# A four-layer graph and mixture-of-experts kernel: x loaded transposed for the first GNN, its second weights applied last

## The reference, cut to what matters

```python
x = x + _L0_gnn_ref(_layernorm(x), adj, adj, W_proj, b_proj, W_gcn, b_gcn)
#   filt = tanh(adj * adj) * (adj > 0)      the 350 largest of each row stay
#   h2   = tanh(h @ W_proj + b_proj)
#   feat = relu(new_adj @ (h2 @ W_gcn) + b_gcn)
x = x + _L0_ffn_ref(_layernorm(x)[None], Wg, bg, bias, W1, b1, W2, b2)[0]
#   gate_logits = x_flat @ Wg + bg + bias   the two best of 8, softmax of the two
#   h = relu(x W1 + b1);  y = h W2 + b2;  weighted sum over the experts
x = x + _L1_gnn_ref(_layernorm(x), adj, L1_gnn_w)
#   deg = sum(adj + I, axis=1), used as deg ** -0.5
```

## Time and profile before

| | us |
|---|---|
| runs of the kernel | 576.0, 575.85, 572.77 (median 575.85) |
| the profiled execution | 571.83 |
| its span, first to last instruction | 570.1 |
| busy in the span: TensorE, VectorE, ScalarE, GpSimd | 487.1, 427.9, 314.2, 252.3 |

### The profile page before, as it was taken

One profiled execution on the slowest core, in us unless ns is written; L12 is line 12 of the kernel. 1 busy time (PEld: TensorE's weight loads), 2 busy tenths in 40 slices (PEclk: granted clock), 3 DMA queues, 4 the chain that ended last, 5 costly groups with the idle time before them and its releaser, 6 DMA issues.

```text
span 570.1 us, 11302 instructions
## 1 busy us (share of the span) xinstructions
PE 487.1 (85%) x3819; PEld 275.4 (48%) x3819; DVE 427.9 (75%) x1065; ACT 314.2 (55%) x522; POOL 252.3 (44%) x275
## 2 busy tenths in 40 slices
PE   1999995879999979998867778889989987898990
PEld 1533333557777745454432233233343226797990
DVE  6897966878999992565778679879977614866674
ACT  0687796966999900120113544456639654466770
POOL 3000002522444440110146189789946575377663
PEclk9999998989999999999957689999999996899996
DMA  8999975200115925011023443200040395869985
GB/s 293 400 422 423 421 274 178 93 1 22 30 28 203 409 58 115 0 42 28 15 75 99 122 118 104 90 2 1 0 143 20 135 356 160 250 182 361 399 299 186
DMA packets 39570, 93.43 MB, mean 164 GB/s; under 512 B 7488, under 2 KB 24944, under 8 KB 35168
## 3 DMA queue, kind: packets, MB, share of 16 engines
q1 hardware_dynamic: 35072, 86.96, 43.4%
q0 software_dynamic: 2272, 4.69, 2.3%
q10 hardware_dynamic: 2176, 1.13, 0.7%
HBM read 69.39 MB, written 21.00 MB: 159 GB/s over the span
## 4 chain that ended last, share of the span: by engine, by line
PE 54%; DVE 20%; DMA 9%; ACT 6%; issue 6%; SPq 3%; POOL 2%; POOLq 0%; DVEq 0%; ACTq 0%
PE ps L1586 9%; DVE A L2393 8%; PE ps L1763 8%; PE ps L1497 7%; PE ps L1514 6%; PE ps L1401 5%; PE ps L1755 3%; DMA R<-in_adj_in 3%; PE ps L1664 3%; DMA A<-w_split 2%; PE ps L1867 2%; PE ps L1611 2%; SPq L812 1%; PE ps L1381 1%; DMA slots_in<-R,A 1%
## 5 line engine op out<-in xcount | busy, mean ns | idle before, releaser
L2393 DVE TENSOR_REDUCE A<-ps 128x1 f32<-128x512 f32 (+3 forms) x160 | 86.1, 601 | 12.3 <-PE ps L1664 11.5
L1302 ACT ACTIVATE A<-ps 128x1024 f32<-128x1024 f32 (+3 forms) x80 | 68.4, 893 | 38.4 <-PE ps L1755 38.2
L1007 POOL TENSOR_TENSOR G<-G,A 128x1024 f32<-128x1024 f32 (+3 forms) x40 | 73.7, 1876 | 8.3 <-ACT A L1302 8.2
L1664 PE MATMUL ps<-A 96*128 96x512 f16 (+3 forms) x160 | 55.1, 382 | 10.3 <-DVE A L2393 4.5
L1401 PE MATMUL ps<-R,G 128*128 128x512 f32 x128 | 59.3, 605 | 1.2 <-DVE G L1967 0.8
L1586 PE MATMUL ps<-A,G 128*128 128x512 f32 x128 | 59.9, 594 | 0.0
L1514 PE MATMUL ps<-R 128*128 128x128 f16 x768 | 49.1, 221 | 7.0 <-DVE x L2085 5.8
L1514 PEld LDWEIGHTS ps<-R 128*128 128x128 f16 x768 | 46.1, 99 | 14.5 <-issue 6.6
L2067 DVE SCALAR_TENSOR_TENSOR R<-R 128x512 f16<-128x512 f32 x64 | 46.7, 752 | 6.8 <-ACT R L1157 6.5
L1867 PE MATMUL ps<-A 128*128 128x128 f16 (+1 forms) x702 | 47.6, 224 | 3.3 <-DMA A<-w_split 3.3
L1155 ACT ACTIVATE R<-ps,b 128x512 f32<-128x512 f32 x64 | 44.0, 688 | 10.6 <-PE ps L1497 9.4
(11 more groups left out here) (311 smaller groups left out, 920.7 us busy)
## 6 DMA issues: line engine op xcount, KB each, us to landing
A<-w_split SPq DMA_DIRECT2D x39, 533.0 KB, 10.2
A<-in_adj_t SPq DMA_DIRECT2D x16, 1024.0 KB, 17.6
slots_in<-xn SPq DMA_DIRECT2D x1, 8320.0 KB, 22.4
R<-in_adj_in SPq DMA_DIRECT2D x7, 1024.0 KB
w_split<-A SPq DMA_DIRECT2D x9, 725.0 KB, 4.0
xn<-in_adj_in SPq DMA_DIRECT2D x5, 1024.0 KB, 12.9
xT<-in_adj_in SPq DMA_DIRECT2D x4, 1024.0 KB, 12.6
A<-in_f_w SPq DMA_DIRECT2D x16, 170.5 KB
```

Source lines behind the costliest of these rows:

```text
L1007: pool.tensor_tensor(total, total, probabilities(n, pair)[:, :, t0:CW], ALU.add).then_inc(s_sum, 1)
L1302: act.activation(probabilities(n, pair)[:, :, t0:CW], ps[:, 2 * pair:2 * pair + 2, t0:CW], ACT.Exp, scale=1.0 / (SQ * SQ * float(HD) ** 0. ...
L1664: last = pe.matmul(ps[:, bank, 0:width], queries(t // TPC, h)[0:KQ, P * (t % TPC):P * (t % TPC) + P], keys(b, h // (NH // NKV))[0:KQ, 0:wi ...
L2393: dve.reduce_max(pm[:, h, t % TPC, b:b + 1], ps[:, bank, 0:width], AX_X).then_inc(s_rmf, 1)
```

## The change

Transposed x (`x_t`, from the host) is loaded beside x, both by chunks, and only chunk 0 precedes adjacency tile 0 on SP's queue; the others go behind tiles 0 to 2. The first layer norm is folded into the projection: the mean by centring the weights' columns (one product with ones, one VectorE instruction), the inverse root by a per-row factor behind the product, so that rows are no longer normalised or transposed there. The aggregation takes h2 itself; the second weights are multiplied behind it, in place of the transposition of the features, and their bias enters as three bf16 parts through one product. The ReLU moves into VectorE's addition. Later chunks' statistics and projections go between the tiles. The narrow operands come in one array, the others in three, issued behind tile 0's tanh. Only 12 row tiles are loaded and summed on ScalarE (10 in the aggregation, two behind it); the degrees of the last four come from TensorE, products with ones over all 16 adjacency tiles, placed in eight groups in the first expert turn and ahead of it, then a copy, a transposition and a copy. In the first turn ScalarE copies outputs 0 and 1 out of their banks (`save_output`), and VectorE's order is written out.

```diff
@@ SP
-            for g in range(NC):
+            def load_x(g):
                 sp.dma_start(x[:, w, :], x_in[:, w, :]).then_inc(s_x[g], 16)
+            def load_transposed_x(g):
+                sp.dma_start(raw_xT[:, CW * g:CW * g + CW], x_t[:, CW * g:CW * g + CW]).then_inc(s_xt[g], 16)
             def load_rows(i):
+                if row_buffer(i) == 2 and i < 3:
+                    sp.wait_ge(s_h2p, 1 + NC)
+                elif i >= 3:
+                    sp.wait_ge(s_rs, 1 + max(k for k in range(i) if row_buffer(k) == row_buffer(i)))
+            ROWS_BEHIND = {4: (0,), 6: (1,), 7: (2,), 9: (3,), 11: (4,), 12: (5,), 14: (6,), 15: (7, 8, 9, 10, 11)}
+            load_x(0)
+            load_transposed_x(0)
             for j in range(NT):
                 sp.dma_start(A[:, j, :], adj_t[j]).then_inc(s_A[j], 16)
+                if j + 1 < NC:
+                    load_x(j + 1)
+                    load_transposed_x(j + 1)
...
-            load_rows(NT - 2)
-            load_rows(NT - 1)
@@ ACT
+            SUMS_BEHIND = {4: (0,), 6: (1,), 7: (2,), 9: (3,), 11: (4,), 12: (5,), 13: (6,), 14: (7,), 15: (8, 9)}
+            FEATURES_BEHIND = {0: 0, 3: 1, 7: 2, 11: 3}
             for j in range(NT):
                 act.activation(fbuf[:, j % FB, :], fbuf[:, j % FB, :], ACT.Tanh).then_inc(s_F, 1)
+                if j in FEATURES_BEHIND:
+                    features_in(FEATURES_BEHIND[j])
+                if j == 0:
+                    for dst, src in small:
+                        act.dma_start(dst, src).then_inc(s_small, 16)
...
             features(s_feat)
-            row_sums(EARLY_ROWS)
+            row_sums(10)
+            row_sums(11)
...
+            scalar_rows(0)
+            high_parts(0)
+            scalar_rows(1)
+            HIGH_BEHIND = {(0, 0): 1, (0, 1): 2, (1, 0): 3}
...
                 if gg == 3:
+                    save_output(0)
+                    act.wait_ge(s_deg, 1)
+                    act.activation(late_sums, ps[:, DEGREE_BANK, 0:P], ACT.Copy).then_inc(s_degr, 1)
+                    save_output(1)
-                    row_sums(NT - 1)
@@ PE
+            pe.wait_ge(s_const, 1)
+            warm(6)
+            pe.wait_ge(s_first, 16)
+            pe.matmul(ps[:, 0, 0:P], full_ones, wmat[:, 0, :], start=True, stop=True).then_inc(s_h2p, 1)
+            def projection(g):
+                pe.wait_ge(s_xt[g], 16)
+                for q in range(TPC):
+                    last = pe.matmul(ps[:, 4 + g, P * q:P * q + P], raw_xT[:, P * (TPC * g + q):P * (TPC * g + q) + P], wmat[:, 0, :],
+                                     start=True, stop=True)
+                last.then_inc(s_h2p, 1)
+            warm(2)
+            pe.wait_ge(s_h2, 1)
+            projection(0)
+            warm(5)
+            projection(1)
+            warm(6)
...
             for j in range(NT - 1):
+                if j in (2, 4):
+                    projection(1 + j // 2)
+                if j % TPC == 0:
+                    pe.wait_ge(s_G, j // TPC + 1)
...
+                    last = pe.matmul(ps[:, 6 + g % 2, P * q:P * q + P], xT[:, P * t:P * t + P], wmat[:, 1, :],
+                                     start=False, stop=True, skip_group_check=True)
...
+            def late_degrees(tiles):
+                for j in tiles:
+                    for c in range(TPC):
+                        last = pe.matmul(ps[32 * c:32 * c + 32, DEGREE_BANK, 0:P], ones[:, :], A[:, j, P * (ROWS + c):P * (ROWS + c) + P],
+                                         start=(j == 0), stop=(j == NT - 1), skip_group_check=True)
...
             rows_back(2)
+            late_degrees(range(0, 2))
+            rows_back(3)
+            late_degrees(range(2, 4))
             rows_again(0)
-            rows_back(3)
-            rows_again(1)
+            late_degrees(range(4, 7))
...
+                if first_turn and SAVED <= gg < 2 * SAVED:
+                    pe.wait_ge(s_saved, gg - SAVED + 1)
@@ DVE
+            def scaled_projection(g):
+                for q in range(TPC):
+                    last = dve.scalar_tensor_tensor(out=G[:, t, :], in0=ps[:, 4 + g, P * q:P * q + P], scalar=rstd[:, t:t + 1],
+                                                    in1=proj_bias, op0=ALU.mult, op1=ALU.add)
...
+            AHEAD_OF = {3: ("scaled", 1), 6: ("stats", 2), 7: ("scaled", 2), 10: ("stats", 3), 11: ("scaled", 3)}
...
+                dve.scalar_tensor_tensor(out=rows(x, g), in0=ps[:, 6 + g % 2, :], scalar=0.0, in1=rows(x, g), op0=ALU.max,
+                                         op1=ALU.add).then_inc(s_x1, 1)
...
+            low(0, 0)
+            low(0, 1)
+            gate_logits()
+            low(0, 2)
+            pick(chain, dve, 1, lg[:, 5], lg)
...
+            add_from_bank(0, 2)
+            low(0, 4)
+            add_from_bank(1, 3)
+            low(0, 5)
+            add_saved(2, 0)
+            add_from_bank(3, 4)
+            low(0, 6)
+            add_saved(4, 1)
+            add_bias2(0, 5)
+            add_from_bank(5, 5)
+            low(0, 7)
+            add_bias2(1, 6)
```

More of the change, by code:

```diff
@@ L363, in program @@
         s_x = [sem(f"x_chunk{g}_loaded") for g in range(NC)]
+        s_xt = [sem(f"transposed_x_chunk{g}_loaded") for g in range(NC)]
         s_first = sem("first_operands_loaded")
+        s_pbias = sem("projection_bias_loaded")
         s_small = sem("small_loaded")
@@ L498, in program @@
         s_pairs = [s_x[2], s_row[2], s_x[0]]
-        pairs_base = [AGAIN, 16 * sum(row_buffer(i) == 2 for i in range(NT)), AGAIN + 16 * (E1 // 2)]
+        pairs_base = [AGAIN, 16 * sum(row_buffer(i) == 2 for i in range(ROWS)), AGAIN + 16 * (E1 // 2)]
         s_wst, s_pair = s_x[0:2], [None, *s_ld0, s_x[3], s_attw]
@@ L1097, in _, with features_in @@
         def _(act):
[L1098 to L1107, removed]
+            act.dma_start(wmat[:, 0, :], w_proj).then_inc(s_first, 16)
+            act.dma_start(proj_bias, b_proj).then_inc(s_pbias, 16)
+            act.wait_ge(s_const, 2)
+            act.activation(cnt[:, 3:4], ones[:, 0:1], ACT.Tanh)
+            def features_in(g):
+                act.wait_ge(s_h2, 1 + g + 1)
+                act.activation(flat0(G, slice(TPC * g, TPC * g + TPC)), flat0(G, slice(TPC * g, TPC * g + TPC)), ACT.Tanh).then_inc(s_G, 1)
             def row_sums(i):
[L1110 removed]
+                act.wait_ge(s_row[row_buffer(i)], 16 * (rows_before(i) + 1))
                 act.activation(row_tile(i), row_tile(i), ACT.Copy, accum_out=sm[:, 11, i:i + 1]).then_inc(s_rs, 1)
[L1113 to L1114 removed]
+            SUMS_BEHIND = {4: (0,), 6: (1,), 7: (2,), 9: (3,), 11: (4,), 12: (5,), 13: (6,), 14: (7,), 15: (8, 9)}
+            FEATURES_BEHIND = {0: 0, 3: 1, 7: 2, 11: 3}
             for j in range(NT):
@@ L1449, in _ @@
                 pe.wait_ge(g_feat, NC)
-                features_back(0)
-                features_back(1).then_inc(g_back, 1)
+                for g in range(2):
+                    features_bias(g)
+                    last = features_back(g)
+                last.then_inc(g_back, 1)
             def rows_back(g):
+                pe.wait_ge(s_x1, g - 1)
+                features_bias(g)
                 pe.wait_ge(s_feat, g + 1)
-                pe.wait_ge(s_x1, g - 1)
                 features_back(g).then_inc(s_ftr, 1)
@@ L1962, in mask @@
                 dve.tensor_scalar(mbuf[:, j % 2, :], fbuf[:, j % FB, :], 0.0, None, ALU.is_gt).then_inc(s_mask, 1)
+            row_statistics_in(0)
+            dve.wait_ge(s_h2p, 1)
+            dve.scalar_tensor_tensor(out=wmat[:, 0, :], in0=ps[:, 0, 0:P], scalar=-1.0 / D, in1=wmat[:, 0, :], op0=ALU.mult,
+                                     op1=ALU.add).then_inc(s_h2, 1)
             square(0)
-            for g in range(NC):
-                dve.wait_ge(s_gp, g + 1)
-                dve.tensor_copy(rows(G, g), ps[:, g, :]).then_inc(s_G, 1)
+            dve.wait_ge(s_pbias, 16)
+            scaled_projection(0)
+            row_statistics_in(1)
+            AHEAD_OF = {3: ("scaled", 1), 6: ("stats", 2), 7: ("scaled", 2), 10: ("stats", 3), 11: ("scaled", 3)}
             for j in range(1, NT):
+                if j in AHEAD_OF:
+                    what, g = AHEAD_OF[j]
+                    if what == "stats":
+                        row_statistics_in(g)
+                    else:
+                        scaled_projection(g)
                 square(j)
@@ L2133, in _, with early_add @@
-            turn(0, True, False)
+            def early_add(n, gg, source):
+                s, g = gg // NC, gg % NC
+                if n:
+                    dve.wait_ge(s_add0, n + 2)
+                for q in range(TPC):
+                    t = TPC * g + q
+                    last = dve.scalar_tensor_tensor(out=x[:, t, :], in0=source[:, P * q:P * q + P], scalar=wcol[:, s, t:t + 1],
+                                                    in1=x[:, t, :], op0=ALU.mult, op1=ALU.add)
+                last.then_inc(s_add0, 1)
```

274 lines of the change are left out of this document (150 added, 124 removed).

## The result

The changed kernel takes 569.15 us (median of five runs, 568.23 to 569.84) beside 574.91 for the kernel before on the same chip (572.77 to 576.0): ratio 0.990, 95% interval 0.9872 to 0.9929. In a second comparison it was 0.9868 (0.9836 to 0.9900). So it is faster by about 1%, 5.8 us. The forecast was 563, a gain of 12.5; the range, 556 to 570, holds the time, but less than half of the gain came. The profiled execution took 569.84 us, its span is 568.1.

A forecast was written before the change was run, and what follows sets the result against it. Prediction: TensorE bounds the aggregation, VectorE the first expert turn behind it. Gains of 8.0 and 4.5 us sum to 12.5, from a median of 575.85 to 563 us; range 556 to 570.

The forecast's parts named there:

- What bounds the kernel: Up to 88.0 us TensorE bounds the aggregation, busy 63.57 of 64.10 us; transfers, share 0.95, are the next limit.
- rival C: SP's queue runs dry at row loads waiting for ScalarE's sums, ten waits of 2.3 us: 584 us, slower; chance 0.05.
- 8.0 us in the aggregation: Aggregation: starts at 13.0 us instead of 23.94 and ends at 80.0 instead of 88.0, 8.0 us gained.
- 1.4 us late for the end: Aggregation's end: the last mask and the bias parts behind it on VectorE come 1.4 us late.
- 4.5 us in the first turn: First expert turn: TensorE enters the repeated experts 45.6 us behind the aggregation instead of 50.1, gain 4.5.
- TensorE enters the repeated experts at 138.06: Kernel before: the first expert turn ends at 138.06 us, 50.1 us behind the aggregation's end at 88.0.
- VectorE as the bound of the turn: Behind the aggregation, first expert turn: VectorE's 26 to 28 us of work set the pace.
- the longest single wait is 3.54 us: Kernel before, first two experts: TensorE's longest wait is 3.54 us, for VectorE's weighted addition.
- The wait that is late next: First expert turn: second bias product waits for VectorE's first bias addition; some 0.05 us allowed at each of a dozen hand-overs.
- Rival B: Before tile 0: TensorE's idling lowers its clock, tile 0 takes 7.9 us for 3.97; 4 us back, 567; chance 0.10.
- Rival A: First expert turn: degree sums cost 0.9 us a tile, TensorE sets the turn, 4.5 us go: 568; chance 0.16.
- Degree sums: TensorE's sums for the last four row tiles: 0.45 us per adjacency tile; nine tiles cost 4.1 us, covered by VectorE.

The follow-up runs named there:

- the tail edit: Changed kernel with row sum 7 behind tile 15's tanh and the maximum of the counts ahead of the bias parts: 568.74 us, ratio 0.9886.

## Why the prediction was wrong where it was

The sum at the mark: 12.5 forecast, 1.75 lost in the aggregation, 2.85 that were never there, 0.4 in the turn, 2.0 at half clock; 5.5 remain.

- *What bounds the kernel* was right at the start: the experiment with all of x ahead of tile 0 moves the aggregation's end by 6.3 us for a start 5.7 us later. The moved loads and the row loads did not run SP's queue dry: the DMA share is 0.93 or more in every stretch of 5 us from 5 to 75 us; rival C falls.
- *8.0 us in the aggregation*: 6.25 came. The start was right to 0.7 us. The term that was too small is "1.4 us late for the end": it is 2.3 us, 79.4 (tile 14's start at 71.46 and two tiles) to 81.7. I had counted VectorE's work there and not ScalarE's order, in which tile 15's tanh stands behind a row sum that waits for its own transfer. With the order exchanged the end is at 80.00, the forecast value, though from a later start: two errors that cancel.
- *4.5 us in the first turn*: minus 0.8. The step that failed is "TensorE enters the repeated experts at 138.06". I had walked to the first hidden product of the loop and subtracted it from the second one of before. The first stands at 135.25, as this row of the kernel before shows, 47.3 us behind the aggregation's end:

```profile
135.25 1.47 PE L1497 MATMUL ps<-G,R 128*128 128x512 f16 x6
```

  After it is 127.74, 46.0 behind the end; I had said 45.6. The walk was good to 0.4 us, in part because errors cancel (cheaper degree sums, the dearer wait below), and the gain that it really forecast was 1.65 us, not 4.5.
- *VectorE as the bound of the turn* held: it is busy 25.14 of the 26.17 us from 100.53 to 126.70, where the prediction had 26 to 28 us of work. But "the longest single wait is 3.54 us" was a misreading: ahead of it TensorE waited 3.97 us for ScalarE's rows in the kernel before. In the changed kernel 2.06 us of that wait are left, and there the tail edit lost its gain:

```profile
95.17 1.12 PE L1381 MATMUL ps<-ident,xn 128*128 128x128 f32 x4 [3.97 <-ACT xn L1175]
```

- *The wait that is late next* was named, "the second bias product, which waits for VectorE's first bias addition", and priced as a hand-over. It was 2.46 us, and the clock that fell behind it takes 1.2 us in the bias product, 1.3 in the hidden and 0.8 in the output product; the last two, 2.0 as far as they reach the mark, were in no term. Rival B had the mechanism, but I put it only ahead of tile 0, where without any warming the aggregation's end came only 0.1 us later. Rival A had priced 568, near the measured 569.15, but its mechanism is not there.
- *Degree sums*: the term is 0.25 us a tile, not 0.45, and leaving them out made the turn longer. *ScalarE's rows* at 7.2 us behind the end: 7.5.
- *The same distance to the end*: 432.2 us from the mark in the profiled execution before, 435.7 after. The former execution, 571.83, was faster than all timed runs of its kernel; the medians show no loss there, and the profiles of all these kernels differ by up to 6 us in that part, so one pair of them does not settle it.

## What to carry to other kernels

Price a wait on TensorE with the products behind it: here 2.5 us of waiting brought 3.3 us of half clock, and closing it by an exchange of two VectorE instructions was worth 4.1 us on a chip where the whole change was worth 6.6. A gain made ahead of a stretch with few products is not passed on by itself: look at what the next stage waits for besides it, here a load issued at a fixed time. When a stretch is measured by hand against a profile, name the same instruction on both sides, by its count in the loop.

## What the runs showed of the hardware that I had not expected

GpSimd's inverse root of 128x4 takes 1.01 to 1.05 us where VectorE is idle or does small work, and 3.29 to 3.33 us beside VectorE's square and mask of 2048 columns (spans on GpSimd are rough in these profiles). In the kernel after, GpSimd in order of time:

```profile
6.31 1.05 POOL L902 TENSOR_TENSOR roots<-variances,neg_half 128x4 f32<-128x4 f32 x1 [4.05 <-DVE variances L2020]
13.66 3.29 POOL L902 TENSOR_TENSOR roots<-variances,neg_half 128x4 f32<-128x4 f32 x1 [6.31 <-DVE variances L2020]
```

It cost little here, since the roots are needed a tile later. And the granted clock can stand at half while TensorE is busy without a gap: 7.85 of 7.85 us at 0.57, above.
